# The 128-column score row of an attention kernel, computed and masked in the third group instead of the second

## The reference

```
mod = (silu(c) @ wmod)               -> shift, scale, gate for both halves
h   = layernorm(x) * (1 + ca) + sa
q, k, v = h @ W_Q, h @ W_K, h @ W_V              16 heads of 64
scores  = q @ k^T / 8, causal mask, softmax over keys
x   = x + ga * (probs @ v @ W_out + b_out)
h   = layernorm(x) * (1 + cb) + sb
x   = x + gb * sum over the 2 best of 8 experts: w_e * (gelu(h @ W1_e + b1_e) @ W2_e + b2_e)
```

## Time and profile before

| | us (or as named) |
|---|---|
| median of three runs | 1894.48 |
| profiled execution | 1895.46 |
| its span | 1893.7 |
| granted TensorE clock, mean share of 2.4 GHz | 0.998 |
| PE busy | 1872.4 (99%) |
| DVE busy | 1667.2 (88%) |
| ACT busy | 1543.3 (81%) |
| POOL busy | 732.2 (39%) |

### The profile page before, as it was taken

How to read it: one execution, slowest core, us unless ns; L and a number is a source line. 1 busy time by engine, 2 the same in 40 slices (tenths; PEclk the granted TensorE clock), 3 DMA queues, 4 the chain that set the end, 5 groups by cost and what they waited for, 6 DMA issues and landing times.

```text
span 1893.7 us, 50578 instructions
## 1 busy us (share of the span) xinstructions
PE 1872.4 (99%) x15326; PEld 1443.0 (76%) x15326; DVE 1667.2 (88%) x4388; ACT 1543.3 (81%) x3664; POOL 732.2 (39%) x1212
## 2 busy tenths in 40 slices
PE   8999999999999999999999999999999999999999
PEld 6777777777777777777777777888888888888887
DVE  7898898898898898898898898989889989999998
ACT  7888888888988988988988988877777777777775
POOL 4445445445445445445445443222222222222221
PEclk9999999999999999999999999999999999999999
DMA  4100000000000000000000002111111111111111
GB/s 126 63 2 1 1 0 1 1 0 1 1 0 1 1 0 1 1 0 1 1 0 1 1 2 90 45 55 52 50 50 50 50 50 50 50 50 50 51 53 53
DMA packets 42622, 50.04 MB, mean 26 GB/s; under 512 B 3160, under 2 KB 24464, under 8 KB 42512
## 3 DMA queue, kind: packets, MB, share of 16 engines
q1 hardware_dynamic: 42256, 48.41, 8.2%
q0 software_dynamic: 256, 0.53, 0.1%
HBM read 44.47 MB, written 4.46 MB: 26 GB/s over the span
## 4 chain that ended last, share of the span: by engine, by line
PE 96%; ACT 2%; issue 1%; DVE 1%; POOL 0%; DMA 0%; ACTq 0%; SPq 0%; DVEq 0%
PE banks L593 15%; PE banks L566 13%; PE banks L580 10%; PE banks L667 6%; PE banks L668 6%; PE banks L669 6%; PE banks L686 6%; PE banks L688 6%; PE banks L687 6%; PE banks L518 6%; PE banks L520 4%; PE banks L519 4%; PE banks L615 2%; PE banks L617 2%; PE banks L616 2%
## 5 line engine op out<-in xcount | busy, mean ns | idle before, releaser
L496 POOL TENSOR_SCALAR probs<-probs,rdenom 128x512 f32<-128x512 f32 (+3 forms) x1024 | 526.2, 537 | 598.6 <-DVE rdenom L1228 598.6
L937 ACT ACTIVATE probs<-probs,neg_max 128x512 f32<-128x512 f32 (+3 forms) x1024 | 564.3, 553 | 80.3 <-DVE neg_max L1219 80.3
L1042 ACT ACTIVATE hidden<-banks,b_cols 128x512 f32<-128x512 f32 x512 | 350.5, 690 | 177.1 <-PE banks L669 176.8
L1219 DVE CUSTOM_DVE_ANT_0 probs<-banks,mask_w 128x512 f32<-128x512 f32 (+3 forms) x1024 | 434.4, 480 | 6.6 <-PE banks L566 0.7
L1395 DVE TENSOR_TENSOR hid_lo<-hidden,hid_hi 128x512 fp32r<-128x512 f32 x512 | 380.6, 755 | 56.3 <-ACT hid_hi L1050 41.6
L482 POOL TENSOR_TENSOR acc<-acc,y_w 128x512 f32<-128x512 f32 x110 | 151.4, 1376 | 462.7 <-DVE y_w L1408 461.0
L593 PE MATMUL banks<-probs_T,v_sb 128*64 128x512 f32 (+3 forms) x2048 | 303.9, 439 | 0.3 <-issue 0.3
L593 PEld LDWEIGHTS banks<-probs_T,v_sb 128*64 128x64 f32 x2048 | 136.1, 136 | 155.2 <-issue 118.3
L1212 DVE COPY probs_T<-banks 128x512 f32<-128x512 f32 (+1 forms) x256 | 234.4, 952 | 18.8 <-PE banks L580 15.6
L580 PEld LDWEIGHTS banks<-ident,probs 64*128 64x128 f32 x5120 | 177.0, 139 | 54.6 <-issue 54.0
L580 PE MATMUL banks<-ident,probs 64*128 64x64 f32 x5120 | 197.0, 226 | 10.1 <-issue 5.4
(11 more groups left out here) (178 smaller groups left out, 3384.0 us busy)
## 6 DMA issues: line engine op xcount, KB each, us to landing
w_rows<-w_kept SPq DMA_DIRECT2D x128, 256.0 KB, 4.5
x_all<-in_L_attn_resid_dram SPq DMA_DIRECT2D x16, 256.0 KB, 2.8
w_raw<-in_L_ffn_W_dram SPq DMA_DIRECT2D x16, 256.0 KB, 4.7
out_dram<-y_result SPq DMA_DIRECT2D x15, 256.0 KB, 2.3
v_sb<-in_L_attn_W_V_dram SPq DMA_DIRECT2D x1, 512.0 KB, 5.9
hidden<-in_L_attn_W_out_dram POOLq DMA_DIRECT2D x2, 256.0 KB, 6.7
v_sb<-in_L_attn_W_Q_dram SPq DMA_DIRECT2D x1, 448.0 KB, 3.9
v_sb<-in_L_attn_W_K_dram SPq DMA_DIRECT2D x1, 448.0 KB, 5.0
```

What stands on the lines that cost most here:

```text
L496: pool.tensor_scalar(part, part, rdenom[:, p % 2, 4 * h + r:4 * h + r + 1], 1.0, ALU.mult, ALU.mult)\
L937: act.activation(part, part, ACT.Exp, bias=neg_max[:, p % 2, col:col + 1], scale=-1.0, accum_out=denom[:, p % 2, col:col + 1]).then_inc(p_ ...
L1042: act.activation(hidden[:, e % 2, c, :], banks[:, c, :], ACT.Gelu, bias=b1_cols[:, e * HC + c:e * HC + c + 1]).then_inc(hid, 1)
L1219: dve.tensor_tensor_reduce(out=probs[:, p % 2, h, at:at + n], in0=S_BANK[u][h][:, col:col + n], in1=mask_w[:, 512 - n:512], scale=-SCALE, ...
```

## The change

Row 0, the one of 128 columns, moves from unit 1 to the end of unit 2. In the second banks (6 and 7) it stands behind row 1, at column 256. The semaphore counts follow: the masks of unit 1 are now numbers 3 and 4 of a pair, those of unit 2 numbers 5 to 8. On ScalarE the order of exponentials becomes: row 3 of both heads, row 2 of both heads, (z and q) row 1 of head 0, (k and values) row 0 of head 0, and last rows 1 and 0 of head 1. Before it was row 3 of both heads, rows 2 and 0 of head 0, row 2 of head 1, (z and q) row 0 of head 1, (k and values) row 1 of head 0, and last row 1 of head 1.

```diff
-UNITS = [[3], [2, 0], [1]]
+UNITS = [[3], [2], [1, 0]]
-ROW_IN_BANK = {3: 0, 2: 0, 0: 384, 1: 0}
+ROW_IN_BANK = {3: 0, 2: 0, 0: 256, 1: 0}
 def masked_at(h, u):
-    return (h, 2 + 2 * h, 6 + h)[u]
+    return (h, 2 + h, 4 + 2 * h)[u]
...
-                            pe.wait_ge(s_masked, (2, 6, 8)[u])
+                            pe.wait_ge(s_masked, (2, 4, 8)[u])
...
-                        pe.wait_ge(s_masked, pair(8, b, p) + (7, 2)[n])
+                        pe.wait_ge(s_masked, pair(8, b, p) + (6, 2)[n])
...
-                                pe.wait_ge(s_masked, done + 6)
+                                pe.wait_ge(s_masked, done + 4)
...
                         exponentials(b, p, 0, 1)
-                        exponentials(b, p, 1, 1, [2])
+                        exponentials(b, p, 1, 1)
...
-                        exponentials(b, p, 1, 1, [0])
+                        exponentials(b, p, 0, 2, [1])
...
-                        exponentials(b, p, 0, 2)
+                        exponentials(b, p, 0, 2, [0])
```

## The result

The changed kernel takes 1906.8 us (median of 6 runs, 1905.94 to 1907.52) against 1894.5 us before (6 runs). The ratio is 1.0066, with a 95% interval of 1.0055 to 1.0076: slower by 12.3 us, where +4.6 was forecast and 1905.5 was the upper end of the range. The profiled execution took 1906.4 us, its span is 1904.6 us, 10.9 longer than before; the granted TensorE clock is 0.999.

A forecast was written before the change was run, and what follows sets the result against it. TensorE was taken to bound the kernel, 96% of the span. Late copies less one gain gave +0.29 us a batch, +4.35 over 15 batches, plus +0.3 in the first: median 1899.1 us, range 1889 to 1905.5.

The forecast's parts named there:

- TensorE, the copy late: Unit 2's first load waits for VectorE's copy: fronts of pairs 3, 5, 0, 2 lose 0.22, 0.09, 0.02, 0.02 us.
- TensorE, the copy in time: Switch to L593 after a 128-column product: 0.06 us gained per front (bounds 0 and 0.06), only pair 6's kept.
- ScalarE, "I take 0": ScalarE: k's high part moves 0.0 to +0.11 us; taken as 0, q's gain set against the longer exponential.
- VectorE and the other waits, cost 0: Eight masks on VectorE take the same time; earlier counts release TensorE from waits long met; cost and gain 0.
- Total: +0.29 us a batch, +4.35 over 15 batches, +0.3 in the first batch; median 1899.1 us.
- Rival 3: No gain switching to L593, 1903.5; later k at pairs 7, 1, 4, 1904; both 1908 us; chance 0.18.
- Rivals 1 and 2: First: T0 copy ready in time, faster, 1889.0 us, chance 0.15; second: wait hides its cost, 1893 to 1896, chance 0.27.
- The chances: Outcomes against the kernel before: faster 0.16, same 0.33, slower 0.51.
- rival 2: TensorE's late load is fetched past its wait or released early: -0.1 to +0.1 us a batch, chance 0.27.
- the low third of the forecast: Lower part of the forecast's own span, +0.2 to +0.45 us a batch (chance 0.40), counted as same.
- The signs: Expected in the changed profile: L566 waiting for `probs_T`, L593 0.89 after the copies, pair 6 0.06 shorter, batch about 71.35.
- T1 copy: ScalarE, end of the pair: one more 128-column exponential ahead, yet it ends before L593's first load; cost 0.

The follow-up runs named there:

- e1: Changed kernel with head 0's two third-unit exponentials exchanged on ScalarE, the 128-column one between q and k; 1897.8 us (before in the same series 1895.6).
- e4: Changed kernel with row 0 ahead of row 1 in the third unit's scores and masks; 1913.25 us (before in the same series 1895.6).
- e2: Kernel before with only ScalarE's order of exponentials taken from the changed kernel; 1901.4 us (before in the same series 1895.6).
- e5: e1 with ScalarE's copy of values moved behind the next, 256-column exponential; 1924.2 us (before in the same series 1895.0).
- e8: e1 with the waits of e6; 1896.6 us (before in the same series 1895.0).
- e6: Kernel before with all 8 masks awaited ahead of T2, leaving the copy-of-values wait alone ahead of T0; 1891.8 us (before in the same series 1895.0).

## Why the prediction was wrong

- *TensorE, the copy late.* Right in mechanism: the load waits for the copy and starts 0.05 after its end, in all late fronts. The price of 0.83 behind the load came out too, but by luck in its parts (0.17 and 0.20 for 0.22 and 0.15). Pair 3 lost 0.22 as forecast, pair 5 0.10 against 0.09. For pairs 0 and 2, where +0.02 each was forecast, it was +0.07 and +0.09: their copies hang on k's low part, which ScalarE had made later. In e1, where it isn't later, these two fronts are 0.02 and 0.01 shorter than before.
- *TensorE, the copy in time.* The size was about right (-0.03 to -0.06; e4 gives it back), the reason was not. The 0.20 ahead of L593 stayed, which was the prediction's other bound and would have meant no gain. The 0.05 came at the second product of row 1, which the prediction held to be equal in either order. That the forecast is right here is luck.
- *ScalarE, "I take 0".* This is the step that failed, in two ways. First k's part: from q to k went from 0.88 to 0.99, as the 0.51 against 0.40 said, and q came only 0.03 to 0.06 sooner. In fronts in time that left k 0.04 to 0.08 later. It should have been priced at that, not cancelled. Second, and larger: I followed k to VectorE's copies, but not the next instruction on ScalarE, the copy of values, to the one that waits for it. T0 had no cover in pairs 3, 4 and 5, and hardly any in 0. Those ends of pairs grew by 0.33 a batch, and e1, e2 and e5 show the link. Both ways together are worth 0.64 of the 0.73: that is what e1 takes back by the order on ScalarE alone.
- *VectorE and the other waits, cost 0.* Right for the masks. But this was where all waits ahead of T0 should have been listed.
- *Total.* Forecast 0.29, measured 0.73 a batch. With pairs 1 and 7 left out, the fronts account for 0.38 of it, of which 0.29 was forecast, and the ends of pairs for 0.33, of which none was. The 0.29 would have been wrong without ScalarE's part too: e1 is only 0.09 above before, because pairs 0 and 2 lose nothing, because the end of pair 3 is 0.05 shorter, and because pair 4 keeps its 0.05. The prediction had k hang on ScalarE and not on TensorE's start, but q's part is released by TensorE's product, and k follows it.
- *Rivals.* Rival 3 named the later k, and gave it 0.11 at the copies of three pairs; its 1908 was near, with the wrong consumer for most of it. Rivals 1 and 2 fell. Ahead of products that don't wait, a load stands 0.17 before its product (610.57, with the product at 610.74), but behind the unmet wait it starts only after the copy's end. The Trainium skill, "TensorE: Matmul & The Clock Gate", Part 3, The mechanism, says that TensorE pulls weight loads ahead of matmuls in flight. No load here was pulled past its wait: in all late fronts it began 0.05 after the copy's end.
- *The chances.* They don't add up as stated: most of rival 2 and the low third of the forecast are 0.39 and not 0.33, which leaves 0.45 for slower.
- *The signs.* The wait of L566 for `probs_T` and 0.88 us from the copies' end to L593 showed, pair 6 was shorter by 0.05, and the T1 copy stayed covered. The batch was not 71.35. k's part stayed within 0.11 of its place only in fronts in time; behind the late fronts it came 0.18 to 0.26 later after the pair's start.

What stays open: of the 12.3 us between the medians, 10.9 show in the two traces; the rest is between profiled executions and medians and wasn't traced. Why the step inside row 1 is longer behind a narrower row isn't known.

## What to carry to other kernels

When a step moves on an engine that isn't the bound, follow each instruction behind it to the one that waits for it, not only the first. Look at the gaps on the bounding engine that are put down to nothing ("issue"). One of them can hide a wait that already has no cover, as the 0.21 ahead of T0 did, and there hundredths count in full. The waits written in the kernel tell which. A small piece of work ahead of a shared buffer's second use is cover for the copy that frees it; moving it turns a 0.11 us margin into a wait, and a saving made elsewhere can be swallowed by the same copy (e8).

## What the runs showed of the hardware

- The start of a weight load behind a wait was 0.05 to 0.06 us after the end of the VectorE copy that released it. With two waits and an empty instruction in a row on TensorE, it was 0.20 to 0.21 after the end of ScalarE's copy (pairs 3, 4 and 5, before and changed). With one wait moved away (e6) it was 0.11, and in pair 4 the next front came 0.11 sooner.
- In a chain of score products on half the rows (L566), the second product of a 256-column row started 0.17 us after the first when a 128-column row stood ahead of it, and 0.12 after it when a 384-column row did (means over 12 batches, fronts in time).
- Going from these products to products on all rows (L593), the load of the latter came 0.20 after the start of the last product, whether that had 256 columns or 128.
